# A fourth PSUM bank in turn for the attended products of a fused attention and feed-forward layer

## The reference

```python
q, k, v = x @ Wq.T + bq, x @ Wk.T + bk, x @ Wv.T + bv       # split in 16 heads
q = softmax(q, axis=-1)          # over the 16 channels of a head
k = softmax(k, axis=-2)          # over the 1024 tokens
state = einsum('bhnd,bhne->bhde', k, v)
out = einsum('bhnd,bhde->bhne', q, state)
x = layernorm(x + (layernorm(out) * ln_g + ln_b) @ Wo.T + bo)
h = gelu(layernorm(x) * g1 + b1) @ ternary(w1).T ...)        # 1024 hidden channels
x = layernorm(x + layernorm(h) @ ternary(w2).T + b2)
```

## Time and profile before

| what | value |
| --- | --- |
| median of 3 runs | 563.69 us (563.56 to 564.07) |
| the profiled execution's own time | 563.79 us |
| its span from the first to the last instruction | 561.9 us |
| mean granted TensorE clock, as a share of full speed | 0.993 |
| TensorE busy | 537.7 us, 96% of the span |
| VectorE, ScalarE, GpSimd busy | 479.8, 482.1, 402.6 us |

### The profile page before, as it was taken

The page is one execution under the profiler, slowest core; times in us unless marked ns, Lnnn a source line. Parts: engine busy times, 40 slices in busy tenths (PEclk is TensorE's granted clock), DMA queues, the critical chain, the costliest instruction groups (busy, mean ns, idle before and its releaser), DMA issues.

```text
span 561.9 us, 10909 instructions
## 1 busy us (share of the span) xinstructions
PE 537.7 (96%) x3550; PEld 495.3 (88%) x3550; DVE 479.8 (85%) x1231; ACT 482.1 (86%) x953; POOL 402.6 (72%) x418
## 2 busy tenths in 40 slices
PE   9999999999999999988899999999999999999990
PEld 9899999898999989878688999999998999999890
DVE  4978898988899898957587899999999999899886
ACT  4845788799979878776989999999999999999983
POOL 4874979877797977476439777766776876686673
PEclk9999999999999999999999999999999999999997
DMA  8440050321705030241110112221122222110002
GB/s 328 169 151 1 1 219 8 139 88 37 263 1 226 2 113 39 73 174 56 76 38 2 39 75 77 77 76 45 33 76 76 77 75 77 41 38 38 37 39 112
DMA packets 11143, 46.52 MB, mean 83 GB/s; under 512 B 1360, under 2 KB 1744, under 8 KB 8912
## 3 DMA queue, kind: packets, MB, share of 16 engines
q1 hardware_dynamic: 10800, 45.29, 22.3%
q10 hardware_dynamic: 288, 0.54, 0.3%
HBM read 29.02 MB, written 16.81 MB: 82 GB/s over the span
## 4 chain that ended last, share of the span: by engine, by line
PE 76%; DVE 10%; ACT 8%; issue 2%; POOL 2%; DMA 1%; ACTq 0%; DVEq 0%; POOLq 0%
PE qps_sps_aps_then_y L1919 21%; PE ring L1895 20%; PE qps_sps_aps_then_y L1680 7%; PE qps_sps_aps_then_y L1766 7%; PE ring L1708 6%; PE qps_sps_aps_then_y L1785 4%; DVE z L1193 3%; PE ring L1837 2%; PE ring L1800 2%; PE ring L1812 1%; PE ring L1850 1%; DVE qsum L1087 1%; DMA x_scratch<-z 1%; PE qps_sps_aps_then_y L1741 1%; PE ring L1609 1%
## 5 line engine op out<-in xcount | busy, mean ns | idle before, releaser
L1919 PE MATMUL qps_sps_aps_then_y<-ff_w_over_xc_lo,ff_a_lo_over_qw 128*128 128x258 f32 x512 | 126.4, 283 | 0.0
L1919 PE MATMUL qps_sps_aps_then_y<-ff_w_over_xc_lo,ff_a_hi_over_xc_lo 128*128 128x258 f32 x512 | 126.1, 283 | 0.0
L1275 DVE SCALAR_TENSOR_TENSOR ff_a_lo_over_qw<-ring,ff_rho,ff_a_hi_over_xc_lo 128x512 fp32r<-128x512 f32 x128 | 92.8, 744 | 16.5 <-ACT ff_a_hi_over_xc_lo L820 15.7
L1895 PE MATMUL ring<-ff_ht_hi_over_qw,t 128*128 128x512 f32 x256 | 104.2, 407 | 0.8 <-DVE ff_ht_lo_over_xc_hi L1267 0.5
L1895 PE MATMUL ring<-ff_ht_lo_over_xc_hi,t 128*128 128x512 f32 x256 | 101.3, 396 | 0.0
L1919 PEld LDWEIGHTS qps_sps_aps_then_y<-ff_w_over_xc_lo,ff_a_hi_over_xc_lo 128*128 128x128 f32 x512 | 96.8, 189 | 3.6
L1919 PEld LDWEIGHTS qps_sps_aps_then_y<-ff_w_over_xc_lo,ff_a_lo_over_qw 128*128 128x128 f32 x512 | 96.7, 189 | 3.4
L802 ACT ACTIVATE ring<-ring,bias 128x512 f32<-128x512 f32 x128 | 83.8, 685 | 8.1 <-PE ring L1895 7.0
L535 POOL TENSOR_TENSOR ff_accp_over_xt_lo<-ff_accp_over_xt_lo,ff_sq_over_ek_et_hi 128x512 f32<-128x512 f32 x64 | 83.3, 1302 | 2.6
L818 ACT ACTIVATE ff_sq_over_ek_et_hi<-ring 128x512 f32<-128x512 f32 x128 | 80.7, 630 | 0.5
L820 ACT CAST ff_a_hi_over_xc_lo<-ring 128x512 fp32r<-128x512 f32 x128 | 79.4, 620 | 0.0
(11 more groups left out here) (180 smaller groups left out, 1617.9 us busy)
## 6 DMA issues: line engine op xcount, KB each, us to landing
x_scratch<-z SPq DMA_DIRECT2D x16, 514.0 KB, 2.9
ff_x_over_w_raw_xc<-x_scratch SPq DMA_DIRECT2D x16, 514.0 KB, 4.8
xt<-in_x_tok_dram SPq DMA_DIRECT2D x8, 1024.0 KB, 4.8
out_dram<-ff_z_over_et_lo SPq DMA_DIRECT2D x15, 512.0 KB, 3.4
xc<-in_x_chan_dram SPq DMA_DIRECT2D x6, 1024.0 KB, 6.9
w_raw<-in_w_dram SPq DMA_DIRECT2D x2, 1024.0 KB, 5.5
ek<-in_x_chan_dram SPq DMA_DIRECT2D x1, 1024.0 KB, 7.8
xc<-in_x_first_dram ACTq DMA_DIRECT2D x1, 512.0 KB, 3.9
```

Of the source, the lines that this page charges most:

```text
L1275: nc.vector.scalar_tensor_tensor(out=ff_a_lo[:, m % DEPTH], in0=ff_bank(k, m), scalar=ff_rho[:, m:m + 1], in1=ff_a_hi[:, m % DEPTH].bitcas ...
L1895: mm = nc.tensor.matmul(ff_bank(k, m), t1[:, c, m * P:(m + 1) * P], h[:, k % 2, c], start=(c == 0 and j == 0), stop=(c == CH - 1 and j == 1))
L1919: last = nc.tensor.matmul(ff_yps[:, t, 0:C + 2], a[:, m % DEPTH, t * P:(t + 1) * P], ff_w2[:, m], start=(m == 0 and j == 0), stop=(m == FC ...
```

## The change

The attended products take bank 1 too. In batches 0 to 5 four banks are used in turn (2, 1, 3, 0), so each bank comes back after four products; before, the distances were two, three or four. In batches 6 and 7 it is three banks in turn (2, 3, 1), before it was two. The waits follow the table: product t waits for the copy of the last product in its bank. The two waits for query centring (`q_sub`, which frees banks 3 and 0) stand at products 2 and 3 instead of 1 and 3.

Since bank 1 is now read by the copies of ScalarE, `state_sum(b, 0)` has one more wait, for copy 5 of batch b - 1, the last product in bank 1 (`y_out` at 8(b - 1) + 6). The first output tile 1 of the feed-forward block waits for copy 5 of batch 7 instead of `m_cent`.

No instruction is added, removed or moved on any engine; only banks and waits differ.

```diff
-ATTEND_AT = (2, 3, 2, 0, 3, 2, 0, 3)
+ATTEND_AT = (2, 1, 3, 0, 2, 1, 3, 0)
+LAST_AT = (2, 3, 1, 2, 3, 1, 2, 3)
...
+        def attend_at(b):
+            return ATTEND_AT if b < NB - 2 else LAST_AT
+
         def a_bank(b, t):
-            n = ATTEND_AT[t] if b < NB - 2 else 2 + t % 2
-            return ff_yps[:, n]
+            return ff_yps[:, attend_at(b)[t]]
...
-                if t in (1, 3) and b + 2 < NB:
-                    pe.wait_ge(q_sub, PAIRS * (b + 2) + (3 if t == 1 else 4))
-                last_use = [n for n in range(t) if ATTEND_AT[n] == ATTEND_AT[t]] if b < NB - 2 else range(t - 1)
+                if t in (2, 3) and b + 2 < NB:
+                    pe.wait_ge(q_sub, PAIRS * (b + 2) + t + 1)
+                last_use = [n for n in range(t) if attend_at(b)[n] == attend_at(b)[t]]
                 wait_for(pe, y_out, T * b + last_use[-1] + 1 if last_use else T * b)
...
                 if n == 0:
                     wait_for(pe, m_cent, CH * b)
+                    wait_for(pe, y_out, T * (b - 1) + 6 if b else 0)
...
                             pe.wait_ge(q_sub, PAIRS * NB)
                             pe.wait_ge(f_out, 3)
-                        elif t == 1:
-                            pe.wait_ge(m_cent, CH * NB)
                         else:
                             pe.wait_ge(y_out, T * NB - 3 + t)
```

## The result

The changed kernel takes 561.15 us (median of 6 runs, 560.16 to 562.54) against 564.10 for the kernel before on the same chip (6 runs, 563.56 to 564.65): the ratio is 0.995, with a 95% interval of 0.994 to 0.996. That is 2.8 us faster (2.3 to 3.4).

What follows compares the result with a forecast made beforehand. TensorE, busy 96% of the span, was taken to bound the kernel. From 563.79 us, 1.5 for batch 7, 1.5 for batch 6, two terms of 0 and 0.10 to the median came off: 560.7 us, range 559.4 to 562.3.

Steps and rivals of the forecast that it cites:

- Batch 7, product 2: Product 2 runs in TensorE's 1.24 us idle instead of waiting for copy 0: 1.5 us gained, bounds 0 and 1.68.
- from copy 0 to the low half: Sign of being right in batch 7: this stretch to VectorE's low half takes some 6.8 us instead of 8.26.
- Batch 6: Stops at products 2 and 7 go; TensorE gains 2.0 us, VectorE limits it: 1.5 taken, bounds 0.8 and 2.0.
- From product 1 to copy 0: Sign: batch 6's product 1 to its store's landing takes 31.1 to 31.5 us if right, still 32.8 if wrong.
- The new wait at the state sums: Copy 5 is 0.93 us late in iterations 3 and 6 only, covered by later idle: cost 0, uncovered 2.1.
- C: Rival: new waits at the state sums are not covered, 2.1 us are paid, time 562.8; chance 0.06.
- D: Rival: slower; state-sum waits cost 2.1 us while only 1.0 of the last batches' gain arrives, 564.8 or more; chance 0.04.
- Batches 0 to 5: Product 2's stops in batches 1 and 2 go, but nothing reaches the end: 0, bounds -0.1 and 0.6.
- VectorE arriving 0.25 earlier is still behind 99.53: Iteration 2: VectorE's residual still starts after GpSimd's operation and is freed at the same moment, so batch 1 gives nothing.
- Rival B: More than forecast: all idle pays, 559.7, or VectorE's residual comes first, its piece 1.9 us shorter; 559.4 to 559.7, chance 0.09.
- iteration 3 as a whole is longer: One of the signs named in advance that would show the prediction wrong; no size given.
- The sum: 563.79 - 1.5 - 1.5 - 0 - 0 = 560.8, less 0.10 gives 560.7 us, 0.5% faster; chance 0.66.

Runs made afterwards that it cites:

- e3: Kernel before with only batch 7 taking bank 1 as a third bank; 562.71 us, ratio 0.9973.
- e4: Kernel before with only batch 6 taking bank 1 as a third bank, with the wait at the last state sum; 562.17 us, ratio 0.997.
- e6: Kernel before, banks untouched, with only the new wait for product 5's copy at the state sums of iterations 1 to 6; 564.46 us, ratio 1.0005.
- e2: Kernel before with the four banks in turn in batches 0 to 5 only, waits at state sums 1 to 6; 564.6 us, ratio 1.0007.
- e5: Changed kernel with ScalarE's two ternary_out calls put behind the copy of product 5 in iterations 3 and 6; 561.17 us, ratio 0.9949.
- e7: Changed kernel with GpSimd's attention_rstd(b-1,1) ahead of tok_c(b,1) at the ends of iterations 1 and 4; 562.19 us, ratio 0.9968.
- e8: Changed kernel with VectorE's statistics of batch 6's product 6 ahead of ff_norm_apply(0,(0,1)); 560.92 us, ratio 0.9945.
- e10: Changed kernel with three one-column memsets on VectorE ahead of the first residual piece at the two turns; 560.13 us, ratio 0.9933.
- e12: Changed kernel with the edits of e10 and e8 together; 560.77 us, ratio 0.994.
- e9: Changed kernel with GpSimd's attention_rstd(b-1,1) ahead of tok_c(b,1) at the ends of iterations 2 and 5; 560.57 us, ratio 0.994.
- e11: Kernel before, banks and order untouched, with the three added VectorE memsets of e10; 563.43 us, ratio 0.9982.
- e1: Kernel before with only batches 6 and 7 taking bank 1 as a third bank; 561.11 us, ratio 0.9949.

## Why the prediction was right, step by step

- **Batch 7, product 2: forecast 1.5, measured 1.5** (e3, 1.0 to 2.0; 1.50 at product 2 in the traces of the changed kernel and e3, some 1.4 behind 289 us with the shorter store taken off). Bounds were 0 and 1.68; product 2 runs without a wait, and from copy 0 to the low half it is 6.88 us instead of 8.26.
- **Batch 6: forecast 1.5, measured 1.7** (e4, 1.0 to 2.3), and 1.6 in the traces where batch 7 changes too. TensorE gained 1.87 at product 7 against 2.0 forecast, VectorE's low halves 0.98 against 258.14 + 1.29 - 258.6 = 0.8, and 1.5 reached the state. From product 1 to copy 0 it is 278.69 - 247.71 = 31.0 us, where 31.1 to 31.5 was forecast to the landing of the store; 0.22 of it is the store, 3.40 us instead of 3.62, which the forecast had at the same length.
- **The new wait at the state sums: forecast 0, measured +0.3** (e6, -0.2 to +0.8; 0.27 in its trace). Place and size were right: 0.83 and 0.89 us in iterations 3 and 6 and none elsewhere, and the idle before line 1816 gone in exchange. Cover was a little short: the transposes came 0.39 late, forecast 0.34, and the second group gave back 0.22 and not all of it, so 0.17 stayed in iteration 3 and 0.15 in iteration 6. Rivals C and D needed 2.1.
- **Batches 0 to 5: forecast 0, measured +0.4 with the wait** (e2, -0.1 to +0.9), +0.34 to +0.65 in the traces. The step "VectorE arriving 0.25 earlier is still behind 99.53" failed. VectorE missed GpSimd by 0.31 us before; less the 1.02 us of the start-up it came 0.27 earlier in the changed kernel (99.84 to 98.55) and GpSimd 0.04 later (99.53 to 98.55). 0.06 us of distance was no margin, and the race flipped, at the second turn too. **Rival B had the flip with the wrong sign.** It counted the 1.9 us that the first piece no longer takes and not that the second piece is held in its place. The rule that it drew on, in the Trainium skill (SBUF, State Buffer, who interferes with whom), has whoever starts first keep the other out for a whole instruction; by that rule, the trace agrees: the next piece takes 2.62 us. VectorE's eight pieces are held once either way; coming first makes GpSimd 0.3 us later, and VectorE's next input comes from GpSimd.
- **A sign of being wrong that did show.** The prediction named "iteration 3 as a whole is longer". It is, by 0.46 us: TensorE's shift, counted from 62 us, goes from -0.29 at 102 to +0.17 at 135. The flip (some 0.35), the end of product 2's gain (0.28) and the state sum's wait (0.17) are in it, less product 2's gain of this iteration (0.32). It is the two forecasts of 0 that failed there, not those of the last two batches.
- **The sum** came out within 0.5 us of the forecast: 1.5 and 1.5 became 1.5 and 1.6 to 1.7, and the 0 for the first six batches and the wait became a loss of 0.3 to 0.65. That the time came so near is in part two small errors of opposite sign, which is luck.

What a flip costs TensorE is shown in the traces by the same alignment. From 106 to 109 us (the first turn) the changed kernel, e5, e7 and e8, flipped there, lose 0.62 to 0.65; e2, e10 and e12, not flipped, lose 0.28, 0.26 and 0.31, which is product 2's gain of 0.28 that ends at GpSimd, as forecast. From 203.6 to 210 us the changed kernel, e2, e5, e7 and e12, flipped, lose 0.34 to 0.43; e8 and e10, not flipped, 0.00 and 0.11. So a flip is some 0.35 us a turn; kernels with nothing changed there differ by up to 0.08. By time alone this is not shown: the intervals of the changed kernel, e8 and e9 overlap, and e10's gain is also there in e11.

## What to carry to other kernels

Price a wait on a bank by the work of the engine that stands still, then ask at every later meeting which engine hands over last: here TensorE's 1.9 us became 1.5 at VectorE's low halves, and that could be read before. When a change moves one engine by a few tenths of a us, look for places where two engines start operations that hold each other within that distance; being first is no gain if the next input comes from the one that was pushed back. A probe that adds an operation needs its own control in the kernel before: e11 took away what e10 seemed to prove by its time.

## What the runs showed of the hardware that I had not expected

**TensorE's clock: an early rise and a dip in mid-run.** Windows of TensorE in the changed kernel, then in the kernel before (window, length, busy (matmuls), granted clock, DMA share, GB/s):

```profile
228.00:235.00 7.00, 7.00 (x50) 1.00 0.01 4
237.90:241.30 3.40, 3.40 (x9) 0.50 0.43 178
243.00:250.00 7.00, 5.73 (x37) 1.00 0.23 81
```

```profile
228.00:235.00 7.00, 7.00 (x52) 1.00 0.00 1
237.90:241.30 3.40, 3.40 (x19) 1.00 0.43 175
243.00:250.00 7.00, 5.47 (x33) 1.00 0.33 116
```

For 3.4 us the granted clock is 0.50, the 1.2 GHz level, though TensorE is busy all the time, and 9 matmuls run where 19 ran before. Matmuls of 512 columns take 0.63 us instead of 0.39. Just before it fell TensorE had been idle for 0.72 us and had run sixteen matmuls of 2 columns in 1.93 us; the kernel before does the same and kept its clock in its profiled execution. The dip costs 1.0 to 1.5 us (the third column of the table) and is there in the profiled executions of eight of the thirteen kernels of the table, with either set of banks, e11 being built on the kernel before.

It goes with the first column. Matmuls of 256 columns in the start-up, two of the kernel before and two of the changed kernel:

```profile
11.15 0.41 PE L1680 MATMUL qps_sps_aps_then_y<-w_hi,xc_lo 128*128 128x256 f32 x1
11.65 0.28 PE L1680 MATMUL qps_sps_aps_then_y<-w_hi,xc_lo 128*128 128x256 f32 x1
```

```profile
8.81 0.41 PE L1683 MATMUL qps_sps_aps_then_y<-w_hi,xc_lo 128*128 128x256 f32 x1
9.35 0.28 PE L1683 MATMUL qps_sps_aps_then_y<-w_hi,xc_lo 128*128 128x256 f32 x1
```

Up to the first change of pace the two executions agree within 0.01 us. The matmuls of 0.41 us start 0.21 us apart, which is the pace of the dip (0.43 for 512 columns there), so the 1.2 GHz level; those of 0.28 us start 0.12 apart, and the changed kernel's execution gets to them 2.3 us sooner. That makes nearly all of its -1.02. In the eight executions with the dip the clock rose 9.2 to 10.7 us after the start, in the five others and in the kernel before 11.5 to 12.2. Why the two go together no run here shows. The first and third columns added are +0.1 to +0.7 in the eight and -0.1 to +0.2 in the five, so over a whole run a third to nine tenths of the dip's cost had been gained at the start.

The runs without a trace fit this: of the runs of before beside e1 to e4, four with a mean clock of 0.987 took 564.70 to 564.81 us, five with 0.993 took 563.31 to 564.05. So it is not the change's doing, but with some 0.5 us by the two columns and 1.0 by these medians it is a sixth to a third of what the change brings, and a single profiled execution with it on one side only would have misled.

**Two engines, less than 0.1 us apart.** Whether `tok_c` or the residual comes first at a turn differed between kernels that are alike up to there: at the first turn the changed kernel, e5 and e8 flipped and e2, the same program so far, did not (GpSimd was 0.03 us ahead); at the second, where the changed kernel, e2 and e8 are still one program, the first two flipped and e8 did not. Each costs some 0.35 us. Every kernel has one profiled execution, so how often it flips in its other runs, and how much of the measured +0.4 of the first six batches is this, is not shown.
